# Silu and tanh in place of sigmoid products in a memory layer's gradient stage, with W1's gradient taken from the normalised input

## What is computed

```python
keys = x @ Wk + bk                                  # x is already normalised
queries = x @ Wq + bq
values = x @ Wv + bv
alr = MAX_ALR * sigmoid(x @ Wlr + blr)
def _lmm(params, h):
    for W, b in params:
        h = h + silu(h @ W + b)
    return h
loss = sum(alr * mean((_lmm(params, keys) - values) ** 2, axis=-1))
grads = grad(loss)                                  # for W1, b1, W2, b2
new = p * (1 - LR * WD) - LR * g / (sqrt(g * g) + EPS)
retrieved = _lmm(new, queries)
```

## Time and profile before

| | |
|---|---|
| median of three runs | 185.67 us |
| the profiled execution | 185.56 us, span 183.7 us |
| busy over the span | PE 169.1, PE's weight loads 135.9, DVE 136.9, ACT 96.6, POOL 25.6 us |
| mean granted TensorE clock | 0.99; 1.00 in all but the last of 40 slices (6 tenths) |
| table loads on ACT | 3, of 1.28 us, at 0.71, 52.99 and 66.54 us |
| first stage | to 52.9 us (new W1 ready); experts from 66.1 us |

### The profile page before, as it was taken

One profiled execution on the slowest core, in us unless ns is written; L12 is line 12 of the kernel. 1 busy time (PEld: TensorE's weight loads), 2 busy tenths in 40 slices (PEclk: granted clock), 3 DMA queues, 4 the chain that ended last, 5 costly groups with the idle time before them and its releaser, 6 DMA issues.

```text
span 183.7 us, 3108 instructions
## 1 busy us (share of the span) xinstructions
PE 169.1 (92%) x1029; PEld 135.9 (74%) x1029; DVE 136.9 (74%) x542; ACT 96.6 (53%) x170; POOL 25.6 (14%) x37
## 2 busy tenths in 40 slices
PE   6879999998999799996999999999999999999970
PEld 6434466656745267995999999998999998999960
DVE  3899998996857827498356979856979866438693
ACT  3258776674574596252725434725435725525511
POOL 2460000000041700024000024100025100002011
PEclk9999999999999999999999999999999999999996
DMA  5992000000000000000000000100000100000100
GB/s 116 306 334 59 5 0 4 0 0 2 0 0 4 2 0 0 4 0 0 0 4 0 2 0 4 57 0 0 5 0 0 57 5 0 0 4 2 57 29 29
DMA packets 3567, 4.99 MB, mean 27 GB/s; under 512 B 352, under 2 KB 2016, under 8 KB 3552
## 3 DMA queue, kind: packets, MB, share of 16 engines
q1 hardware_dynamic: 3552, 4.81, 8.4%
HBM read 3.76 MB, written 1.05 MB: 26 GB/s over the span
## 4 chain that ended last, share of the span: by engine, by line
PE 71%; DVE 18%; issue 4%; ACT 3%; POOL 1%; DMA 1%; DVEq 0%; ACTq 0%; POOLq 0%
PE bank L380 65%; DVE stats L873 4%; PE bank L388 4%; DVE mv L876 2%; DVE xn_tok L886 2%; POOL rstd L333 1%; DMA x_tok<-in_x_dram 1%; DVE xn_tok L1042 1%; PE bank L546 1%; DVE xnT L1137 1%; DVE vpe L881 1%; PE bank L537 1%; DVE h_tok L886 1%; ACT sig L809 1%; ACT L790 1%
## 5 line engine op out<-in xcount | busy, mean ns | idle before, releaser
L1137 DVE SCALAR_TENSOR_TENSOR xnT<-bank,w_tok,xnT 128x128 f32<-128x128 f32 x112 | 31.5, 345 | 21.4 <-PE bank L380 20.8
L333 POOL TENSOR_TENSOR rstd<-vpe,minus_half 128x4 f32<-128x4 f32 (+1 forms) x25 | 22.1, 891 | 114.9 <-DVE vpe L881 103.8
L380 PE MATMUL bank<-z_hi,fW_hi 128*128 128x512 f32 x64 | 27.8, 434 | 0.3 <-ACT alrT L683 0.3
L380 PE MATMUL bank<-z_lo,fW_hi 128*128 128x512 f32 x64 | 25.0, 393 | 0.0
L380 PE MATMUL bank<-z_hi,fW_lo 128*128 128x512 f32 x64 | 25.0, 390 | 0.0
L380 PEld LDWEIGHTS bank<-fW_sb,sig 128*128 128x128 f32 x192 | 23.1, 192 | 0.7
L380 PE MATMUL bank<-fW_sb,sig 128*128 128x128 f32 x192 | 23.4, 275 | 0.0
L809 ACT ACTIVATE sig<-bank,early_sb 128x512 f32<-128x512 f32 x24 | 16.0, 685 | 9.8 <-PE bank L380 9.8
L380 PEld LDWEIGHTS bank<-fW_sb,k_tok 128*128 128x128 f32 x160 | 19.5, 191 | 0.8
L380 PEld LDWEIGHTS bank<-fW_sb,h1T 128*128 128x128 f32 x160 | 19.4, 191 | 0.8
L380 PE MATMUL bank<-fW_sb,k_tok 128*128 128x128 f32 x160 | 19.6, 275 | 0.0
(11 more groups left out here) (134 smaller groups left out, 271.0 us busy)
## 6 DMA issues: line engine op xcount, KB each, us to landing
fW_raw<-in_fW_dram SPq DMA_DIRECT2D x1, 1024.0 KB, 8.7
x_tok<-in_x_dram SPq DMA_DIRECT2D x3, 256.0 KB, 4.8
out_dram<-xn_tok SPq DMA_DIRECT2D x3, 256.0 KB, 2.5
early_sb<-in_early_dram SPq DMA_DIRECT2D x1, 268.0 KB, 3.7
late_sb<-in_late_dram SPq DMA_DIRECT2D x1, 264.0 KB, 5.3
x_tok<-in_x_dram SPq DMA_DIRECT2D x2, 128.0 KB, 2.6
b_raw<-in_late_dram SPq DMA_DIRECT2D x16, 4.0 KB
out_dram<-xn_tok SPq DMA_DIRECT2D x2, 128.0 KB, 1.9
```

What stands on the lines that cost most here:

```text
L333: pool.tensor_tensor(rstd[:, ln, where], vpe[:, ln, where], minus_half[:, 0:where.stop - where.start], ALU.pow).then_inc(rstd_ready[ln], 1)
L380: return pe.matmul(out_, lhsT, rhs, start=start, stop=stop)
L1137: last = dve.scalar_tensor_tensor(out=y_tok[:, t, :], in0=bank[Y_BANK[m % len(Y_BANK)]][:, i * P:(i + 1) * P], scalar=w_tok[:, t, e:e + 1] ...
```

## The change

- Layers 1 and 2 of the first stage: ACT computes silu from the product in one instruction and, in a second one from the same bank, tanh of half the argument; DVE's products s1 and s2 are gone. The step n1 or n2 makes 1 - sigmoid from tanh as 0.5 - 0.5 tanh. The rate alr is kept as tanh too, dp uses (tanh + 1) * e, and the factors left out are taken into the constants of adam. The halved biases are made by one small ACT instruction (half_cols).
- The dummy silu before the retrieval is gone, and the first dummy instruction is a silu.
- W1's gradient: bank 4 now accumulates the normalised x's tokens times dz1. In the tail ACT copies that sum to xw1, PE multiplies it with Wk and adds the bias row of k times the row of b1's gradient (steps "row" and "wg1"), into bank 3. The token-major copies of k are gone, and a strided load of bk as a row is added on SP's queue.
- Blocks 2 and 3 of x are normalised inside waves 0 and 1, behind layer1; the step x works one block less ahead and stands between h1 and n2 in the wave; the fw steps are one wave later on DVE.
- Sigmoid buffers become dz1T and dz2T.

```diff
-        WAVE = ["dh1", "dz2", "z2", "h1", "n2", "z1", "alr", "gw2", "dz1", "v", "gw1", "k", "n1", "kp", "x", "fw"]
+        WAVE = ["dh1", "dz2", "z2", "h1", "x", "n2", "z1", "alr", "gw2", "dz1", "v", "gw1", "n1", "kp", "fw"]
-               "v": 1, "gw1": -1, "k": 0, "n1": 1, "kp": 2, "x": 3, "fw": 1}
+               "v": 1, "gw1": -1, "n1": 1, "kp": 2, "x": 2, "fw": 0}
...
-                            ("gw1", last), ("q", 2), ("q", 3))
+                            ("row", 0), ("gw1", last), ("wg1", 0), ("q", 2), ("q", 3))
...
+            sp.dma_start(bk_row[:], early[:, bk_at:bk_at + 1].rearrange("p o -> o p"),
+                         allow_slow_non_contiguous=True).then_inc(bk_row_in, 16)
...
+            def bias_row():
+                pe.wait_ge(gbs_ready, 1)
+                pe.wait_ge(dh1_done, NB)
+                pe.transpose(bank[6][0:1, 0:P], gbs[:, 0:1], ident[:]).then_inc(gb1_mm, 1)
+
+            def w1_gradient():
+                pe.wait_ge(xw1_ready, 1)
+                pe.wait_ge(gb1_ready, 1)
+                pe.wait_ge(bk_row_in, 16)
+                mm(bank[3][:, 0:P], wk_sb, xw1[:], start=True, stop=False)
+                mm(bank[3][:, 0:P], bk_row[:], gb1_row[:], start=False, stop=True).then_inc(gw1_mm, 1)
...
-            feature_major_x(2)
...
-                "gw1": lambda b: gradient(bank[4][:, 0:P], k_tok, dz1_tok, b, "dz1", gw1_mm),
+                "gw1": lambda b: gradient(bank[4][:, 0:P], xn_tok, dz1_tok, b, "dz1", xw1_mm),
...
-            def sigmoid(b, product, source, into, bias, s):
+            def silu_and_tanh(b, product, source, bias, half_bias, into, ready, tanh_into, read, tanh_ready):
+                slot = b % NSIG_RING
                 act.wait_ge(product, b + 1)
-                act.activation(cut(into, b), source[:], ACT.Sigmoid, bias=bias).then_inc(s, 1)
+                act.activation(cut(into, b), source[:], ACT.Silu, bias=bias).then_inc(ready, 1)
...
+                act.activation(tanh_into[:, slot * BLOCK:(slot + 1) * BLOCK], source[:], ACT.Tanh, scale=0.5,
+                               bias=half_bias).then_inc(tanh_ready, 1)
...
             kT_out(0)
-            sig1_out(0)
+            act.wait_ge(halves_ready, 1)
+            s1_out(0)
             xnT_out(1)
+            kT_out(1)
             nsig1_out(0)
-            kT_out(1)
-            xnT_out(2)
-            fw1_high(0)
...
-            act.activation(warm[:], minus_half[:, 0:1], ACT.Silu).then_inc(table_ready, 1)
...
             def layer1(b):
-                dve.wait_ge(sig1_ready, b + 1)
-                dve.scalar_tensor_tensor(out=cut(s1, b), in0=bank[3][:], scalar=col(B1),
-                                         in1=cut(sig1, b), op0=ALU.add, op1=ALU.mult).then_inc(s1_done, 1)
-                dve.wait_ge(s1_done, b + 1)
+                dve.wait_ge(s1_ready, b + 1)
                 dve.tensor_tensor(cut(h1T, b), cut(s1, b), cut(kT, b), ALU.add).then_inc(h1_done, 1)
...
-            x_norm(2)
             dve.wait_ge(early_in, 16)
             for w in range(NB + 1):
                 if w < NB:
                     layer1(w)
+                if w < 2:
+                    x_norm(w + 2)
                 if w:
                     layer1_back(w - 1)
-                else:
-                    x_norm(NB - 1)
...
-                if w < NB - 1:
-                    fw1_low(w)
+                if 0 < w < NB:
+                    fw1_low(w - 1)
...
+            dve.wait_ge(dz1_done, NB)
+            dve.tensor_reduce(gbs[:], gb[:], AX_X, ALU.add).then_inc(gbs_ready, 1)
...
-            run(adam(w1n[:], w1_sb, bank[4][:, 0:P], adam_tmp[:, 2, :], adam_tmp[:, 3, :], w1n_ready))
+            run(adam(w1n[:], w1_sb, bank[3][:, 0:P], adam_tmp[:, 2, :], adam_tmp[:, 3, :], w1n_ready))
```

More of the change, by code:

```diff
@@ L218, in wave @@
                     yield what, b
-        TURNS = [("x", 1), ("x", 2)]
+        TURNS = [("x", 1)]
         FIRST_BANK = (7, 5)
         for w in range(NB + 1):
-            TURNS += [step for step in wave(w) if step[0] in ("x", "k", "h1", "dz2", "dz1")]
+            TURNS += [step for step in wave(w) if step[0] in ("x", "h1", "dz2", "dz1")]
         PARTS = [(TB * b, TB) for b in range(NB - 1)] + [(T - TB, TB // 2), (T - TB // 2, TB // 2)]
@@ L283, in col, with half_col @@
             return cols[:, i:i + 1]
+        def half_col(i):
+            return half_cols[:, cols_at - blr_at + i:cols_at - blr_at + i + 1]
         def bank3(i):
@@ L683, in copy, with one_less @@
                 act.activation(dst, src, ACT.Identity, **kw).then_inc(s, 1)
-            def sigmoid(b, product, source, into, bias, s):
+            def silu_and_tanh(b, product, source, bias, half_bias, into, ready, tanh_into, read, tanh_ready):
+                slot = b % NSIG_RING
                 act.wait_ge(product, b + 1)
-                act.activation(cut(into, b), source[:], ACT.Sigmoid, bias=bias).then_inc(s, 1)
-            def one_less(b, sig, into, ready, read, s):
-                slot = b % NSIG_RING
-                act.wait_ge(ready, b + 1)
+                act.activation(cut(into, b), source[:], ACT.Silu, bias=bias).then_inc(ready, 1)
                 if b >= NSIG_RING:
                     act.wait_ge(read, b - NSIG_RING + 1)
-                act.activation(into[:, slot * BLOCK:(slot + 1) * BLOCK], cut(sig, b), ACT.Identity,
-                               scale=-1.0, bias=1.0).then_inc(s, 1)
+                act.activation(tanh_into[:, slot * BLOCK:(slot + 1) * BLOCK], source[:], ACT.Tanh, scale=0.5,
+                               bias=half_bias).then_inc(tanh_ready, 1)
+            def one_less(b, tensor, tanh_ready, s):
+                slot = b % NSIG_RING
+                where = slice(slot * BLOCK, (slot + 1) * BLOCK)
+                act.wait_ge(tanh_ready, b + 1)
+                act.activation(tensor[:, where], tensor[:, where], ACT.Identity, scale=-0.5,
+                               bias=plus_half[:]).then_inc(s, 1)
             def transposed(kind, b, into):
@@ L729, in qT_out, with bias_row_out, w1_gradient_out @@
                 copy(cut(qT, b), bank[Q_BANK[b % len(Q_BANK)]][:], qT_ready, bias=col(BQ))
-            def alr_out(b):
-                sigmoid(b, alr_mm, bank[1], alrT, blr_b, alr_ready)
-            act.wait_ge(half_ready, 1)
-            act.activation(gb_tmp[:, 0:1], minus_half[:, 0:1], ACT.Sigmoid).then_inc(table_ready, 1)
+            def bias_row_out():
+                act.wait_ge(gb1_mm, 1)
+                copy(gb1_row[:], bank[6][0:1, 0:P], gb1_ready)
+            def w1_gradient_out():
+                act.wait_ge(xw1_mm, 1)
+                copy(xw1[:], bank[4][:, 0:P], xw1_ready)
+            def alr_out(b):
+                act.wait_ge(alr_mm, b + 1)
+                act.activation(cut(alrT, b), bank[1][:], ACT.Tanh, scale=0.5,
+                               bias=half_cols[:, 0:1]).then_inc(alr_ready, 1)
+            act.wait_ge(half_ready, 2)
+            act.activation(gb_tmp[:, 0:1], minus_half[:, 0:1], ACT.Silu).then_inc(table_ready, 1)
             for h in range(2):
@@ L933, in layer2 @@
             def layer2(b):
[L935 to L938 removed]
+                dve.wait_ge(s2_ready, b + 1)
                 dve.wait_ge(hv_done, b + 1)
```

76 lines of the change are left out of this document (40 added, 36 removed).

## The result

The changed kernel takes 189.75 us (median of four runs, 189.59 to 189.84), the kernel before 185.70 beside it: a ratio of 1.0219, 95% interval 1.0201 to 1.0237. The prediction was 189.0 us in a range of 187.2 to 190.8, slower. Beside the last experiments the changed kernel ran again: 189.74.

The account below looks back on a forecast made before the run. PE's in-order queue bounds waves 1 to 3, with little slack in ACT and DVE; before that DVE is late. Terms 1.3 + 1.6 + 0.0 - 0.25 + 0.1 + 0.4 + 0.1 = 3.25, called +3.3: median 189.0 us, range 187.2 to 190.8.

Parts of the forecast that it names:

- to dh1 of block 0: Wave 0: copies queued on ACT make alr late, so PE starts dh1 at 21.7 instead of 20.42 us, +1.3.
- wave 1: From dh1 of block 0 to that of block 1: PE idles 1.6 us until ACT has copied h1, +1.6.
- wave 2: Loses k's transposes, 0.44 us, and pays 0.48 for dz1's transposes of block 1 behind ACT's queue: 0.0.
- wave 3: Saves 0.44 us for k and loses 0.2 because DVE's dz2 of block 3 is later than PE: -0.25.
- to the last gradient: Tail, from dh1 of block 3 to its W1 gradient: the added row transpose costs +0.1 us.
- last gradient to silu: Tail, W1 gradient's start to first silu: sum's copy, two small products and q steps take 5.4 us for 5.01, +0.4.
- retrieval and the rest: w2's product for the queries finds PE still in the third rz1 product instead of idle, +0.1 us.
- The two waits: PE idles at x's transposes in waves 0 and 1 until ACT has copied h1, 1.85 and 1.6 us.
- The table load: Hand-over to the retrieval: removing the load and its dummy is worth about 0.7 us, the load itself 1.28.
- A: Rival: copies come in time and bank 7 waits cost nothing, so the kernel is faster, -2.0, 183.7 us; chance 5%.
- C: Rival: silu and tanh share no table, so 16 loads come on ACT, about 205 us; chance 4%.
- D: Rival: PE's idle time before dh1 lowers TensorE's clock to 1.2 GHz, some 3 us more, 192 us; chance 6%.

Follow-up runs that it names:

- silu and tanh alone: The changed kernel with x's normalisation in the waves and the new W1 gradient taken back: 188.17 us, 1.0117 of the kernel before.
- the reordered kernel: The changed kernel with x normalised ahead of the waves, the bias row's product first, tanh apart from silu and another wave order: 183.88 us, 0.9897 of before.

## Why the prediction was right, and where it missed

The waits stood where it put them, and the cause was the one it named, ACT's queue with x's transposes behind h1's. The time was 0.75 us short, the sum of the span 1.1 (3.3 for 4.4); that the median was nearer than the sum is luck, of which the last point tells.

| term | predicted | measured |
|---|---|---|
| to dh1 of block 0 | +1.3 | +1.80 |
| wave 1 | +1.6 | +1.59 |
| wave 2 | 0.0 | +0.01 |
| wave 3 | -0.25 | -0.35 |
| to the last gradient | +0.1 | +0.10 |
| last gradient to silu | +0.4 | +0.80 |
| retrieval and the rest | +0.1 | +0.45 |
| sum, span | +3.3 | +4.4 |

- **What bounds the kernel.** That PE is bound by its queue with little slack behind it was right, and so was that DVE's work taken away (6.2 us counted, 5.2 less by the pages) was worth nothing in this order: silu and tanh alone cost 0.99 us to the first silu and 1.59 to the end. In the reordered kernel, which has the same lighter DVE, dh1 of block 0 comes 0.96 us sooner than before; how much of that is DVE's is not shown.
- **Wave 0.** The two waits were predicted as 1.85 and 1.6 and measured as 1.83 and 1.39. Of the 0.5 us that were missed, 0.21 is the start (z1 of block 0 at 9.75 for 9.54; the second half of x landed later in this execution, and with tanh behind the copies z1 began at 9.45). The term that was mis-sized is the slope: "a copy in SBUF 0.52", a price taken from a copy whose bias is a plain number, where n1 and n2 now take theirs from a tensor. They take 0.71 us for 0.63 and come 0.61 apart: 0.09 more each, twice ahead of alr. The last 0.1 lies in steps that were each out by less than 0.1. (The Trainium skill, ScalarE: Activation LUTs, What ACT_TABLE_LOAD costs, has 93 ns for such an operand; the trace agrees with 0.08 to 0.09.)
- **Waves 1 to 3.** Their sums came out nearer than their terms, which is luck too. In wave 1 the wait was 0.2 shorter than predicted, and PE was busy 0.2 longer (9.19 for 8.99). In wave 2 PE waited 0.23 for the copy of dz1, where 0.48 was laid out. In wave 3 the 0.2 for DVE's dz2 didn't show as idle time of PE; it waited 0.79 us for the copy of dz1, for 0.69 before.
- **Which step does the harm.** The prediction put the tanh "ahead of the copies that PE waits for" first, and the neighbouring transposing steps second. Moving tanh behind the copies won nothing, moving x won 2.6 us. Its own lay-out of wave 0 had alr as the last link; the sentence that summed it up was wrong, the sum wasn't.
- **Tail.** The two products were taken as 0.45 of PE's queue between bounds of 0.25 and 0.7; they took 0.83, outside the bounds. The mistake was to price four passes of 128 columns as in a dense row of transposes, 0.11 each. Here the first product waits for ACT's copy and the weight load of each next one begins only with it, so a pass took 0.21, in the row's product as in the other. Turned round, the order gives 0.5 back on PE and 0.6 to the first silu.
- **The table load** was worth less than 0.7: 0.46 to the first silu, and of this perhaps a third at the end. The price of the load itself, 1.28 us read from its row, was right.
- **Retrieval.** I had 0.1 for w2's product behind rz1's. PE's product for w2 starts 1.38 us after the first silu (59.73) for 1.06 before (55.46, after 0.38 of idle time). As foreseen, PE comes to it straight from rz1's products; but these hold it for 2.08 us (57.65 to 59.73), and the silu is only 0.70 behind their start where it was 1.28 with the load, so it is 0.32 and not 0.1. The remaining 0.13 was not followed up.
- **The load of bk.** Costed at nothing, and right for the time: SP's queue was held by it for 7.03 us (5.54 to 12.57), but the 16 loads of b2 behind it wait for POOL's zeroes anyway (until 14.5, before 13.7), 2 us after SP was free again, so nothing was lost.
- **The rivals.** A failed at the point it named: the copies came 1.83 and 1.39 us late. C is out: there are two table loads, at 0.72 us and before the gelus, so silu and tanh share a table. D did not happen where it was put; PE idled as much as foreseen with the clock at 1.00. But the clock does fall in other executions, at the start: there the first four passes took 3.53 and 3.65 us for 1.95, 1.6 to 1.7 us lost where D was priced at 3.
- The predicted median was 189.0 with 0.1 for the difference between the execution and the median; the span grew by 4.4 and the median by 4.05, and this difference of 0.35 made the miss smaller. Of it 0.23 is that the profiled execution lay 0.14 below the median before (185.56 for 185.70) and 0.09 above it in the change (189.84 for 189.75), the rest that the execution was 1.86 us longer than its span before and 1.74 in the change.

## What to carry to other kernels

Where several engines walk one written order, as here, an edit's cost can be set by its place in the queue more than by its work (nearly the same parts took 189.75 us in one order and 184.64 in another): lay the new order out by hand with start-to-start distances from the trace, follow it to the last input of the next stage, and move the steps before judging the idea. Two steps that use one PSUM bank should not be neighbours in PE's queue, and what the next stage waits for (here alr) goes ahead of what can wait. A wait that gets shorter proves nothing: look whether the next one grew. Work taken from the busiest engine is only won if the tail that replaces it is shorter.

## What the runs showed of the hardware

- **TensorE's clock at the start.** When the first x landed at 4.0 or 4.1 us for 3.1, PE stood idle 1.05 and 1.25 us behind its warm-up transposes, and the granted clock then averaged 0.54 to 0.60 of full from 8 to 12 us: it was at its lower level of 1.2 GHz (0.50) from about 8.4 to 11.8 in the one trace and 8.2 to 11.6 in the other; four passes of 512 columns took 3.53 and 3.65 us for 1.95. Later idle times of PE of 1.83 and 1.39 us in the change left it at 1.00.
- **A product with one partition of depth** and 128 columns took 0.41 us of PE's queue, a full one 0.42 in the change. Behind the row's product, and with the next weight load running beside it, the full one took 0.32.
- **A bias from a tensor** on a 512-wide ACT copy in SBUF: 0.71 us for 0.63. From a PSUM bank it is 0.69 (k and q) for 0.60 (copies without a bias).
- **A load of 128 separate numbers** as one row held the issuing queue for 7.03 and 7.37 us, where a load of 1024 KB in rows held it 0.43.
